# Sandwich layer on one core: the spills of q, k and the decayed k laid out in 2-KB rows

## The reference

```
x = x + layernorm(attention(layernorm(x)))
x = x + layernorm(ffn(layernorm(x)))

# attention: 16 heads of 32 features, chunks of 128 tokens, state S per head (32 x 32)
q, k, v = split(x @ w_qkv.T + b_qkv)
inter  = (q * decay_q) @ S
intra  = ((q @ k.T) * dmask) @ v
S      = lam_c * S + (k * decay_k).T @ v
out    = (inter + intra) @ w_out.T + b_out
# ffn: weights rounded to fp8 (e4m3), 512 -> 1536 -> 512
down(silu(gate(x)) * up(x))
```

## Time and profile before

| | |
|---|---|
| median of 3 runs | 988.04 us (987.9 to 988.89) |
| the profiled execution | 988.57 us, its span 986.8 us |
| PE busy | 958.7 us (97%) |
| DVE, ACT, POOL busy | 690.4, 509.1, 687.6 us |
| moved by DMA | 159.88 MB in 297642 packets |
| packets under 512 B / under 2 KB / under 8 KB | 141632 / 272832 / 297408 |
| granted clock of PE over the span | 0.995 |

### The profile page before, as it was taken

One profiled execution on the slowest core, in us unless ns is written; L12 is line 12 of the kernel. 1 busy time (PEld: TensorE's weight loads), 2 busy tenths in 40 slices (PEclk: granted clock), 3 DMA queues, 4 the chain that ended last, 5 costly groups with the idle time before them and its releaser, 6 DMA issues.

```text
span 986.8 us, 22045 instructions
## 1 busy us (share of the span) xinstructions
PE 958.7 (97%) x8498; PEld 708.9 (72%) x8498; DVE 690.4 (70%) x1359; ACT 509.1 (52%) x985; POOL 687.6 (70%) x837
## 2 busy tenths in 40 slices
PE   8999999999998999999999999999999999999996
PEld 6777777786766777767677676767767676776764
DVE  7999998875887675767667576766757676665422
ACT  3656665565654544636354463635446363544522
POOL 2699998986775675849567584947758594775733
PEclk9999999999999999999999999999999999999999
DMA  9899899999983983847658284766828476512200
GB/s 322 210 290 265 255 276 293 277 254 297 229 207 88 202 180 56 196 93 163 131 127 176 61 194 94 163 128 129 191 48 193 92 165 125 127 52 43 41 26 22
DMA packets 297642, 159.88 MB, mean 162 GB/s; under 512 B 141632, under 2 KB 272832, under 8 KB 297408
## 3 DMA queue, kind: packets, MB, share of 16 engines
q1 hardware_dynamic: 296672, 157.86, 67.4%
q10 hardware_dynamic: 864, 0.61, 0.2%
HBM read 82.93 MB, written 41.94 MB: 127 GB/s over the span
## 4 chain that ended last, share of the span: by engine, by line
PE 57%; DVE 17%; POOL 11%; issue 10%; ACT 4%; DMA 1%; POOLq 0%; DVEq 0%; SPq 0%; ACTq 0%
PE bank L892 17%; PE bank L874 12%; PE bank L767 8%; PE att L767 7%; PE bank L782 7%; POOL att_pool L1059 4%; DVE stats L1326 3%; DVE p L1367 3%; DVE state_hl L1397 3%; DVE w_pool L1460 2%; POOL rstd L998 2%; ACT w_pool L596 2%; POOL w_pool L1077 2%; PE att L851 1%; DVE state L1386 1%
## 5 line engine op out<-in xcount | busy, mean ns | idle before, releaser
L874 PE MATMUL bank<-f_pool,gate_q 128*128 128x256 f16 x1536 | 185.0, 274 | 4.3 <-ACT w_pool L596 3.8
L874 PE MATMUL bank<-f_pool,up_q 128*128 128x256 f16 x1536 | 183.7, 273 | 1.5
L892 PE MATMUL bank<-down_q,w_pool 128*128 128x512 f16 x768 | 168.3, 379 | 0.0
L874 PEld LDWEIGHTS bank<-f_pool,gate_q 128*128 128x128 f16 x1536 | 147.4, 98 | 27.0 <-ACT w_pool L596 6.5
L874 PEld LDWEIGHTS bank<-f_pool,up_q 128*128 128x128 f16 x1536 | 149.4, 98 | 22.4 <-DVE w_pool L1460 5.1
L1059 POOL TENSOR_TENSOR att_pool<-p,att_pool 128x512 f16<-128x512 f32 x128 | 145.7, 1159 | 28.0 <-ACT att_pool L548 27.9
L1460 DVE SCALAR_TENSOR_TENSOR w_pool<-bank,us_t,w_pool 128x256 f32<-128x256 f32 x192 | 84.1, 479 | 112.5 <-ACT w_pool L596 54.7
L995 POOL TENSOR_TENSOR rstd<-mv,eps_t 128x1 f32<-128x1 f32 (+1 forms) x112 | 30.1, 269 | 181.3 <-DVE mv L1329 181.3
L892 PEld LDWEIGHTS bank<-down_q,w_pool 128*128 128x128 f16 x768 | 74.0, 98 | 86.9
L1077 POOL TENSOR_TENSOR w_pool<-w_pool 128x512 f16<-128x512 f32 x96 | 111.3, 1165 | 28.0 <-ACT w_pool L602 27.9
L548 ACT CAST att_pool<-p 128x512 f16<-128x512 f32 x128 | 75.7, 615 | 62.4 <-DVE p L1367 62.3
(11 more groups left out here) (145 smaller groups left out, 1826.4 us busy)
## 6 DMA issues: line engine op xcount, KB each, us to landing
xr<-in_x SPq DMA_DIRECT2D x32, 512.0 KB, 4.6
dram_qk<-qk_hl SPq DMA_DIRECT2D x64, 256.0 KB, 3.7
att_pool<-dram_qk SPq DMA_DIRECT2D x64, 256.0 KB, 5.3
f_pool<-dram_qk SPq DMA_DIRECT2D x64, 256.0 KB, 5.6
dram_kd<-kd_hl SPq DMA_DIRECT2D x32, 256.0 KB, 2.9
dram_v<-vv SPq DMA_DIRECT2D x32, 256.0 KB, 3.7
qn_pool<-dram_qk SPq DMA_DIRECT2D x32, 256.0 KB, 6.2
out_x<-w_pool SPq DMA_DIRECT2D x32, 256.0 KB, 2.3
```

What stands on the lines that cost most here:

```text
L874: ins = nc.tensor.matmul(b[:, j * TOK:(j + 1) * TOK], w[:, k, o * P:(o + 1) * P], x1_hl[:, v % 2, part, k], start=(k == 0 and part == 0), ...
L892: ins = nc.tensor.matmul((b_gate, b_up)[t][:, :], h_hl[:, part, k, t * P:(t + 1) * P], down_q[:, k], start=(k == 0 and part == 0), stop=(k ...
```

## The change

The DRAM tensors are laid out so that a partition's whole row of 1024 float16 values (2 KB: four groups of 256 tokens) stays together. `dram_qk` gets the order [unit, q or k, hi or lo, d (32), j (4), 1024], with d outermost, `dram_kd` the order [unit, hi or lo, partition (128), 1024].

- `spill_q`, `spill_k` and `load_q` walk the DRAM side as "d j f -> j d f": 4 x 32 rows of 1024 values. Before it was 128 x 4 rows of 256.
- `spill_kd` becomes 128 rows of 1024 values.
- `load_stack` has pieces of 64 or 32 partitions with rows of 4096 values (8 KB, all of a partition's heads), two for q and three for k: 5 copies per unit in place of 8. The heads in a stack now stand in the order 4 j + g, and `scores` picks them so.
- `load_kt` turns the same bytes, but the columns of `kt` now stand as 4 p + g. The state products therefore take as weights every fourth column (`k_cols[:, a, g]`: 128 columns, 8 bytes apart); before, 128 adjacent ones.

```
-        dram_qk = nc.dram_tensor("dram_qk", [units, 2, 2, KT, P, TOK], F16, kind="Internal").ap()
-        dram_kd = nc.dram_tensor("dram_kd", [units, 2, KT, P, TOK], F16, kind="Internal").ap()
+        dram_qk = nc.dram_tensor("dram_qk", [units, 2, 2, DH, HG, KT * TOK], F16, kind="Internal").ap()
+        dram_kd = nc.dram_tensor("dram_kd", [units, 2, P, KT * TOK], F16, kind="Internal").ap()
...
             def spill_q(n):
                 sp.wait_ge(q_lo_d, 2 * n + 2)
                 for part in range(2):
-                    sp.dma_start(dram_qk[n, 0, part].rearrange("k p t -> p k t"), qk_hl[:, part, 0:KT]
-                                 ).then_inc(q_spilled, 16)
+                    sp.dma_start(dram_qk[n, 0, part].rearrange("d j f -> j d f"),
+                                 qk_hl[:, part, 0:KT].rearrange("p k t -> p (k t)")).then_inc(q_spilled, 16)
...
             def spill_kd(n):
                 sp.wait_ge(kd_lo_d, 2 * n + 2)
                 for part in range(2):
-                    sp.dma_start(dram_kd[n, part].rearrange("k p t -> p k t"), kd_hl[:, part]
+                    sp.dma_start(dram_kd[n, part], kd_hl[:, part].rearrange("p k t -> p (k t)")
                                  ).then_inc(kd_spilled, 16)
...
-            def load_stack(s, which, parts):
+            def load_stack(s, which, pieces):
                 sp.wait_ge(*((k_spilled if which else q_spilled), 32 * (s + 1)))
-                for r in range(4):
-                    sp.dma_start(stacks[s % 2][DH * r:DH * (r + 1), which],
-                                 dram_qk[s, which, parts[r]].rearrange("g (j d) t -> d (g j) t", d=DH)
+                for row, first, last in pieces:
+                    sp.dma_start(stacks[s % 2][DH * row:DH * (row + last - first), which].rearrange("d h t -> d (h t)"),
+                                 dram_qk[s, which, first:last].rearrange("s d j f -> (s d) (j f)")
                                  ).then_inc(stack_in[s % 2], 16)
...
             def load_q(s):
                 for part in range(2):
-                    sp.dma_start(qn[:, s % 2, part], dram_qk[s, 0, part].rearrange("k p t -> p k t")
-                                 ).then_inc(q_in[s % 2], 16)
+                    sp.dma_start(qn[:, s % 2, part].rearrange("p k t -> p (k t)"),
+                                 dram_qk[s, 0, part].rearrange("d j f -> j d f")).then_inc(q_in[s % 2], 16)
...
-                    load_stack(s, 1, (0, 0, 1, 1))
+                    load_stack(s, 1, ((0, 0, 2), (2, 1, 2), (3, 0, 1)))
...
-                    load_stack(s, 0, (0, 1, 0, 1))
+                    load_stack(s, 0, ((0, 0, 2), (2, 0, 2)))
...
+                    k_cols = kt[s % 2][:, c].rearrange("t s (f g) -> t s g f", g=KT)
                     for g in range(KT):
                         for n, (a, b) in enumerate(((0, 0), (0, 1), (1, 0))):
                             ins = nc.tensor.matmul(b_t[1][:, g * P:(g + 1) * P],
-                                                   kt[s % 2][:, c, a, g * P:(g + 1) * P], v_halves[:, heads(g), b],
+                                                   k_cols[:, a, g], v_halves[:, heads(g), b],
                                                    start=(n == 0), stop=(n == 2))
```

More of the change, by code:

```diff
@@ L324, in spill_k @@
                 for part in range(2):
-                    sp.dma_start(dram_qk[n, 1, part].rearrange("k p t -> p k t"), qk_hl[:, part, KT:2 * KT]
-                                 ).then_inc(k_spilled, 16)
+                    sp.dma_start(dram_qk[n, 1, part].rearrange("d j f -> j d f"),
+                                 qk_hl[:, part, KT:2 * KT].rearrange("p k t -> p (k t)")).then_inc(k_spilled, 16)
             def spill_kd(n):
@@ L368, in load_kt @@
                 sp.dma_start_transpose(kt[s % 2].rearrange("p t s d -> p t (s d)"),
-                                       dram_kd[s].rearrange("s g p t -> (s g p) t")).then_inc(kt_in[s % 2], 16)
+                                       dram_kd[s].rearrange("s p (g t) -> (s p g) t", g=KT)).then_inc(kt_in[s % 2], 16)
             def load_unit(s, step=None):
@@ L788, in scores @@
                 if c == 0 and half == 0:
-                    pe.wait_ge(stack_in[s % 2], 128 * (s // 2 + 1))
+                    pe.wait_ge(stack_in[s % 2], 80 * (s // 2 + 1))
                     if s == 0:
@@ L795, in scores @@
                         ins = nc.tensor.matmul(b_s[g % 2][:, j * P:(j + 1) * P],
-                                               stacks[s % 2][:, 1, HG * g + j, c * P:(c + 1) * P],
-                                               stacks[s % 2][:, 0, HG * g + j, c * P:(c + 1) * P], start=True, stop=True)
+                                               stacks[s % 2][:, 1, KT * j + g, c * P:(c + 1) * P],
+                                               stacks[s % 2][:, 0, KT * j + g, c * P:(c + 1) * P], start=True, stop=True)
                     ins.then_inc(score_mm, 1)
```

## The result

The changed kernel takes 1085.76 us (median of 4 runs, 1084.64 to 1086.65) against 987.97; the ratio is 1.0987, 95% interval 1.0973 to 1.1001: 97.8 us slower. The forecast was 1061, in a range of 1030 to 1100. The profiled execution took 1086.65 us, its span 1084.9.

The account below looks back on a forecast made before the run. PE was taken to bound the kernel, busy 97% of the span. 988.57 us profiled + 67 in the lead + 3 after it + 2 clock + 0 weights = 1061.6, less 0.5 to the median: 1061 us, range 1030 to 1100.

Parts of the forecast that it names:

- Four engines: Spills of q and k and `load_q`, with 4 indices outermost, would run on 4 DMA engines, not 16; chance 0.84.
- The rate: Each of the four engines would move 26.25 GB/s, so a 256-KB copy of q or k takes 2.50 us.
- The q and k buffers are single, and SP's order ties everything into one ring: In the lead, a closed cycle of waits through the k spill would take 22.3 us a round against PE's 15.66.
- my chain: The lead's cycle of DMA, landing, ACT, POOL and issue times: 22.3 us a round, 16.4 for the kernel before.
- Where in the lead: Lead +67 us: first three rounds 0, round 3 2.4, rounds 4-9 40, rounds 10-13 19, loads 1.5 and 4.
- After the lead: +3: Behind the lead, the k spill of unit 15 would cost 3 us (ends 0 and 6), `load_q` in the slots 0.
- SP: 0: On SP's queue, three copies fewer per unit at about 0.5 us of issue would be worth nothing: SP waits.
- Clock: +2: PE's clock, lower after rests, would cost 2 us, in the first slots only.
- Weights and slots: State products with every fourth column as weights would cost 0 (0.67 us per 12), and slots keep their length.
- DMA share "well under 0.86": Sign of being right: DMA share in the lead falls well under 0.86 though DMA is the bound.
- The three with sixteen engines: Rivals with copies on 16 engines: nothing gained, 988 us (0.05); faster, 985 or 986 (0.04); slow weights, 1005 (0.03).
- PE at 1.2 GHz throughout: Rival: rests hold PE at 1.2 GHz through lead rounds, 31.3 us each, +157, 1145 us in all; chance 0.04.

Follow-up runs that it names:

- The padded run: Kernel with 128 rows outermost, plus an unused 33rd DRAM row behind each 32, so q and k copies walk 4 x 32 rows: 1085.47 us, ratio 1.0983.

## Why the prediction came out as it did

**Four engines: right.** The padded run gives the whole loss back, and windows with such copies alone have a share of 0.26 with 102 GB/s (four), and of 0.52 with 203 GB/s (eight). By the Trainium skill (DMA: Bandwidth & Descriptors, "Why a DMA increments its semaphore by 16 and not by 1") four engines for 4 outermost and eight for 8 were to be expected, and the runs agree. No row of before could show it.

**The rate: right.** "65536 B / 26.25 = 2.50 us" per copy was taken from windows in which 16 engines work, and it carries over: 102 GB/s from four engines are 25.5 each, q and k of a unit 10.2 us against 10.0. The 79 GB/s of one window misled my later expectations.

**"The q and k buffers are single, and SP's order ties everything into one ring": the buffers failed as the cause, SP's order is part of it.** Second buffers bring 0.9 us, with ACT's queue 3 more. The chain does run through this wait (a spill of k in 13.29 us, and 7 us of ACT, DVE and issue to the next one), but without it the round is as long. What the runs show instead is a sum of two. The work in the rings of the four engines is 17.6 us a round, which was my lower end ("if only the ring's total work counted", +45 in the lead): with the spills off SP's queue the rounds are 17.7 and the lead +48, with second buffers too 17.6 and +43. With the spills on SP's queue 2.7 us a round come on top: SP is held in the transposes about as long as the four engines work on the spills, what stands behind goes out late, and for a moment hardly anything moves. How these 2.7 us divide wasn't tried, nor whether the single buffers of kd and v have a part in them. The sum is 20.3, where my chain said 22.3. The chain was too long from the start: for the kernel before it gave 16.4 us, and rounds of 15.66 without a gap allow no more than 15.66. That the lead still came out at 67 is luck in part.

**Where in the lead: sum right, parts not.** Measured against the starts of the same rounds before: +7.5 for `bo` ahead of round 2 (forecast 0), +5.5 in rounds 2 and 3 (2.4), +33 in rounds 4 to 9 (40, plus 1.5 for loads), +20 in rounds 10 to 13 (19 + 4). That is 67, and 67 was said.

**"After the lead: +3": this is the step that failed.** It was +31. I counted only the spill of k of unit 15, at 2.9 us. Shown by the runs: the spills of units 14 and 15 5 to 8 us, `load_q` 6 us (3 of it in the lead, though two runs with the same lead differ there by 2), and 17 us that appear even where neither is on four engines. SP is 13 us further behind PE when the lead ends, with the rings full, so that the first attention finds its operands late (+19 in the changed kernel from the last product of the lead to `attend(0, 0)`), and then the turned output of unit 0 (+10). I had taken the end of the lead as a clean cut. How the 17 us divide between late spills, held transposes and clock wasn't tried, and their cause stays open.

**"SP: 0": wrong in kind.** Copies fewer are indeed worth nothing, but SP doesn't only wait for semaphores: it is held in its own issue, 12.82 us against 3.00 in the same round. Taking the spills off its queue gave 20 us back.

**Clock: +2, undecided.** 48 products after a rest take up to 8.26 us in place of 5.40; over the lead that makes 17 us of longer PE work, in rounds that wait for x anyway. No run separates what of it counts.

**Weights and slots: right.** 0.67 us per 12 products, and in the slots PE is busy 39.68 of 40 us.

**DMA share "well under 0.86": wrong.** It was 0.74 to 1.16 in the lead at 185 to 214 GB/s. With copies alone it told four engines (0.26 and 0.27), with transposes among them it did not: while SP was held in one it went to 1.94, and at 10 GB/s it still said 1.18. Bytes per us were the reading to trust, over windows short enough to hold one kind of copy.

**Rivals.** The three with sixteen engines are out (1085.47 us with only the 4 restored); so is PE at 1.2 GHz throughout: the windows of the lead show a clock of 0.79 to 1.00.

## What to carry to other kernels

When a DRAM layout changes, look at the outermost dimension of the walk that is left after merging before looking at row length: here 128 or 4 rows outermost was the whole difference between 988 and 1085 us, and 512-B against 2-KB rows was none. The cure keeps the long rows: put the dimension that spreads over partitions outermost (partition-major, 987.85 us). And when a phase ends with its queues full, cost the next phase too: about a third of this loss was booked there.

## What the runs showed of the hardware

- Four DMA engines alone move 102 GB/s in the lead (the changed kernel, 152 to 157 and 196 to 201 us), eight 203, sixteen with 2-KB rows and longer 397 to 420: 25 to 26 each. One stretch with four had 79 on average, 61 to 102 in single microseconds; why is not known.
- SP is held in the issue of two DMA transposes for 2.6 to 3.0 us in most rounds with 16-engine spills, 5.8 to 6.3 with eight, 9.7 to 12.6 with four, and 6.6 to 7.1 with four when the spills are on ACT's queue; where loads of unit 0 come on top it is 5.0 to 5.5, 8.7 to 9.5, 10.6 to 12.8 and 12.3 to 13.6. That it waits for room in the busy rings fits this, but was not measured by itself.
- Rows four times as long and a quarter as many for q, k and kd, with the same 16 engines, changed nothing: 0.9997.
- Weights 8 bytes apart changed nothing in 336 products: 0.9998.
- In the changed kernel's lead, after rests of 3.1 to 9.4 us, PE's next 48 products of 256 columns took 6.5 to 8.3 us in place of 5.40, in windows with a granted clock of 0.79 to 0.85.
